# Attention scores issued for two heads at a time in the first stage of a two-layer decoder

## The reference, cut to what matters

```python
def _L0_attn_ref(x, Wq, Wk, Wv, rel_bias_table, ln_gamma, ln_beta):   # H = 16 heads of 8
    q, k, v = (einsum('bsd,ed->bse', x, W) split into heads for W in (Wq, Wk, Wv))
    attn = softmax(einsum('bhqd,bhkd->bhqk', q, k) * d_model ** -0.5)
    attn = attn + rel_bias[None]
    out = einsum('bhqk,bhkd->bhqd', attn, v), heads joined
    return layernorm(out) * ln_gamma + ln_beta
x = x + _L0_attn_ref(_layernorm(x), ...)
```

## Time and profile before

| | us |
|---|---|
| median of three timed runs | 643.53 |
| profiled execution | 639.99 |
| its span, first to last instruction | 638.0 |
| TensorE matmul busy in it | 542.6 (85%) |
| VectorE, ScalarE, GpSimd busy | 421.6, 327.5, 193.3 |

### The profile page before, as it was taken

The page is one execution under the profiler, slowest core; times in us unless marked ns, Lnnn a source line. Parts: engine busy times, 40 slices in busy tenths (PEclk is TensorE's granted clock), DMA queues, the critical chain, the costliest instruction groups (busy, mean ns, idle before and its releaser), DMA issues. The chain is left out here.

```text
span 638.0 us, 12873 instructions
## 1 busy us (share of the span) xinstructions
PE 542.6 (85%) x4890; PEld 334.9 (53%) x4890; DVE 421.6 (66%) x1037; ACT 327.5 (51%) x809; POOL 193.3 (30%) x288
## 2 busy tenths in 40 slices
PE   1777888999999999778896479988997989999995
PEld 1533344344555656455464355665665766655553
DVE  5595674642563554788559865757556567689894
ACT  1424355556577574586642535553664547363440
POOL 3554200312263443332620031001113122335663
PEclk9875799999999999889998789999998999999997
DMA  8600000000030000000166005300000000300301
GB/s 289 258 2 2 2 3 3 1 3 2 1 134 0 2 1 1 2 2 1 43 174 234 1 2 165 103 3 2 4 3 2 3 3 1 134 2 0 133 2 33
DMA packets 25815, 27.92 MB, mean 44 GB/s; under 512 B 18177, under 2 KB 22794, under 8 KB 24858
## 3 DMA queue, kind: packets, MB, share of 16 engines
q1 hardware_dynamic: 25754, 27.10, 12.7%
HBM read 22.14 MB, written 4.75 MB: 42 GB/s over the span
## 5 line engine op out<-in xcount | busy, mean ns | idle before, releaser
L785 POOL TENSOR_TENSOR A_l0x_prob<-A_l0x_prob,A_l0x_inverted_sums 128x256 f32<-128x256 f32 (+1 forms) x32 | 26.2, 840 | 61.7 <-DVE A_l0x_inverted_sums L896 61.7
L785 POOL TENSOR_TENSOR B_l0x_prob<-B_l0x_prob,B_l0x_inverted_sums 128x256 f32<-128x256 f32 (+1 forms) x32 | 27.1, 868 | 46.6 <-DVE B_l0x_inverted_sums L896 46.5
L879 DVE TENSOR_REDUCE A_l0x_nmax<-A_banks 128x2 f32<-128x256 f32 (+1 forms) x32 | 16.3, 551 | 26.9 <-PE A_banks L954 26.9
L2054 PE MATMUL A_banks<-A_moe_xT,w_moe_rows 128*128 128x512 f32 x72 | 34.0, 599 | 0.0
L2054 PE MATMUL B_banks<-B_moe_xT,w_moe_rows 128*128 128x512 f32 x72 | 33.3, 599 | 0.0
L299 DVE TENSOR_REDUCE B_l0a_nmax<-B_banks 128x2 f32<-128x512 f32 x32 | 21.4, 686 | 17.4 <-PE B_banks L226 17.3
L299 DVE TENSOR_REDUCE A_l0a_nmax<-A_banks 128x2 f32<-128x512 f32 x32 | 21.4, 685 | 12.0 <-PE A_banks L226 11.8
L333 ACT ACTIVATE A_l0a_expT<-A_banks 128x512 f32<-128x512 f32 x32 | 18.5, 599 | 21.0 <-PE A_banks L263 21.0
L803 ACT ACTIVATE B_l0x_prob<-B_banks,B_l0x_nmax 128x128 f32<-128x128 f32 x64 | 26.0, 421 | 6.0 <-DVE B_l0x_nmax L879 6.0
L803 ACT ACTIVATE A_l0x_prob<-A_banks,A_l0x_nmax 128x128 f32<-128x128 f32 x64 | 26.0, 427 | 1.2 <-DVE A_l0x_nmax L879 1.2
L820 ACT ACTIVATE B_l0x_probT<-B_banks 128x384 f32<-128x384 f32 x32 | 15.8, 493 | 21.0 <-PE B_banks L966 21.0
(11 more groups left out here) (610 smaller groups left out, 1605.1 us busy)
## 6 DMA issues: line engine op xcount, KB each, us to landing
w_toeplitz_rows<-in_toeplitz_rows SPq DMA_DIRECT2D x1, 3072.0 KB, 15.8
w_moe_rows<-in_moe_rows SPq DMA_DIRECT2D x1, 2304.0 KB, 8.8
w_l1x_rows<-in_l1x_rows SPq DMA_DIRECT2D x1, 2048.0 KB, 8.6
A_l1x_values<-A_l1a_v_tokens SPq DMA_DIRECT2D x4, 512.0 KB, 3.2
A_l1x_v_groups<-A_l1x_values SPq DMA_DIRECT2D x16, 128.0 KB, 3.1
B_l1x_values<-B_l1a_v_tokens SPq DMA_DIRECT2D x4, 512.0 KB, 3.4
B_l1x_v_groups<-B_l1x_values SPq DMA_DIRECT2D x16, 128.0 KB, 3.3
w_l0x_vo_rows<-in_l0x_vo_rows SPq DMA_DIRECT2D x1, 1024.0 KB, 8.9
```

Source lines behind the costliest of these rows:

```text
L785: ins = pool.tensor_tensor(pair, pair, bcast(rz[:, g % 2, i, :], 2, n), ALU.mult)
L879: ins = dve.tensor_reduce(nmax[:, b, i, 2 * c:2 * c + 2], lane.banks[:, 0:2, at:at + n], AX, ALU.max, negate=True)
L2054: pe.matmul(hidden_bank(k)[:, :], w["moe_w3" if which else "moe_w1"][:, ORDER[i], part, :], xT[:], start=True, stop=True).then_inc(s_h.sem, 1)
```

## The change

Two new functions issue two heads at a time, and alternate between them: first half of head h, first half of head h + 1, second half of h, second half of h + 1. The two heads lie in opposite row halves and go to two banks. `tensor_S_pair` is used for the first sequence's scores, `tensor_E_pair` for all shifted scores. Each waits once, for both banks. The second sequence's scores keep `tensor_S`. The number of turns per engine and lane stays; a turn that issued the odd head's matmuls now issues none. The table of turns is another one for every engine.

```diff
+    def tensor_S_pair(self, pe, m):
+        if m:
+            pe.wait_ge(*self.s_mx(m))
+        for c in range(SB):
+            for h in (m, m + 1):
+                ins = pe.matmul(self.score_bank(h)[:, c * S:(c + 1) * S], self.q(0, h, c * P, P), self.k(0, h, 0, S),
+                                start=(c == 0), stop=True, skip_group_check=True)
+                if c == SB - 1:
+                    ins.then_inc(self.s_s.sem, 1)
+
+    def tensor_E_pair(self, pe, u):
+        b, h = divmod(u, H)
+        if h == 0:
+            pe.wait_ge(*self.s_q(16 * self.G * (b + 1)))
+        if u:
+            pe.wait_ge(*self.s_p(u))
+        for c in range(SB):
+            for i in range(2):
+                ins = pe.matmul(self.exp_bank(u + i)[:, c * S:(c + 1) * S], self.k(b, h + i, c * P, P), self.q(b, h + i, 0, S),
+                                start=(c == 0), stop=True, skip_group_check=True)
+                if c == SB - 1:
+                    ins.then_inc(self.s_e.sem, 1)
...
-            a.tensor_S(pe, u)
-            if u % 2:
+            if u % 2 == 0:
+                a.tensor_S_pair(pe, u)
+            else:
                 yield
                 transpose_stack(4 * SB + u // 2)
...
-            if n < U:
-                a.tensor_E(pe, n)
+            if n < U and n % 2 == 0:
+                a.tensor_E_pair(pe, n)
...
     "tensor":
-        "A4 W1 A3 W1 A25 B2 A1 B1 A3 B1 A6 B2 A2 B1 A1 B2 A2 B2 A4 B1 A1 B2 A5 B3 A3 B1 ...
+        "A4 W1 A7 W1 A20 B1 A4 B1 A1 B1 A3 B1 A3 B1 A3 B1 A1 B1 A1 B1 A3 B1 A2 B2 A3 B1 ...
     "vector":
-        "A3 W1 A1 W1 A4 W6 A3 B1 A4 B1 A1 B1 A15 B1 A13 B1 A2 B3 A2 B1 ...
+        "A3 W1 A1 W1 A2 W1 A2 W2 A2 W2 A1 W1 A5 B1 A1 B1 A1 B1 A11 B1 A15 B1 A1 B3 A4 B1 ...
     "gpsimd":
-        "A12 B3 A4 B13 A10 B2 ...
+        "A12 B1 A3 B2 A1 B13 A11 B1 ...
     "sync":
-        "A1 W13 B1 A2 B2 L1 ...
+        "W3 A1 W10 B1 A2 B2 L1 ...
```

More of the change, by code:

```diff
@@ L2358 @@
     "tensor":
[7 rows of a table removed]
-    "vector":
[8 rows of a table removed]
-    "scalar":
[4 rows of a table removed]
[8 rows of a table added]
+    "vector":
[9 rows of a table added]
+    "scalar":
[5 rows of a table added]
     "gpsimd":
-        "A12 B3 A4 B13 A10 B2 A2 B3 A4 B1 A1 B1 A1 B1 A2 B1 A1 B2 A2 B1 A1 B7 A3 B2 A3 B2 A1 B8 A8 B3 A3 B3 A1 B1 A2 B3 A1 B2 A2 B2 A2 B1 A10 B4 A1 B10 A1 B2",
+        "A12 B1 A3 B2 A1 B13 A11 B1 A1 B1 A1 B2 A1 B1 A2 B1 A1 B1 A1 B1 A2 B1 A1 B2 A2 B1 A1 B6 A1 B2 A1 B1 A3 B2 A1 B1 A1 B7 A8 B2 A2 B2 A1 B2 A2 B2 A1 B3 A1 "
+        "B1 A1 B2 A7 B1 A4 B3 A1 B1 A1 B9 A1 B1 A1 B2",
     "sync":
-        "A1 W13 B1 A2 B2 L1 A6 L1 A3 B7 A1 B3 A2 B2 A1 B1",
+        "W3 A1 W10 B1 A2 B2 L1 A6 L1 A3 B5 A1 B5 A2 B2 A1 B1",
 }
```

## The result

| | before | changed |
|---|---|---|
| median of the timed runs, us | 644.13 (643.41 to 645.62, 4 runs) | 619.78 (619.46 to 621.6, 4 runs) |
| profiled execution, its span | 639.99, 638.0 | 619.47, 617.5 |
| TensorE's mean granted clock in it | 0.946 | 0.954 |

The ratio is 0.9625 (95% interval 0.9598 to 0.9652): 24 us faster, where 4 were forecast and 10 were the end of the range. VectorE, ScalarE and GpSimd are as busy as before (424.6, 323.5 and 192.1 us); TensorE is busy 529.0 us for 542.6. For the experiments further down, medians are those of all executions, while ratios compare only executions within 1.5% of the fastest of their kernel, so the two don't divide into each other.

What follows compares the result with a forecast made beforehand. TensorE was taken to bound the kernel from 112 us on. 3.6 - 1.0 - 0.5 + 1.5 = 3.6 us off 643.53 gave 640.0 us; range 638 to 642, 8 in 10 within 634 to 647.

Steps and rivals of the forecast that it cites:

- (c): Every engine's turns re-ordered through the whole program: 1.5 us gained at the start, 0 later than 170 us.
- the rest of the table: Turns later than 170 us: same code, small shifts, sign unknown; 0 us, bounds of 5 us either way.
- if the lead changes after 170 us, the table is the cause: Sign in the changed trace: work from 170 us on should keep the same lead of 3 to 4 us.
- The start: Lane A's opening turns, before its scores: it can begin its scores earlier, 1.5 us gained, upper bound 3.31.
- the cover that I counted on: Lane A's first scores: VectorE must still do sixteen reductions, so 1.5 us was taken, not the upper bound 3.31.
- (a): First-stage scores on TensorE: two heads alternated in a pair share places, 3.6 us gained, bounds 0 and 6.4.
- (b): First-stage scores: a pair waits for both banks; 1.0 us lost at A's reductions (gap 0.47 for 0.24), 0.5 at exponentials.
- The loss of a second bank: Rival, lane A's first scores and its loop from 52 to 110 us: 4.9 us slower, 648.4 us; chance 0.10.
- ScalarE's idle time: Sign before the first stage's exponentials: 21.0 and 14.3 should stay or fall; growth over 5 means lost banks decide.
- Hidden already: Rival, first-stage scores: the chip already overlaps adjoining heads, a gain of 1 meets a loss of 1, 643.5 us; chance 0.14.
- the table gains more: Rival: the start gives 3.3 us, the places after 170 us some 2 more, 636 us; chance 0.20.
- the 3.5 us between the profiled execution and the timed median: Whole run: the timed median 643.53 lies 3.5 us above the profiled 639.99; the same gain was taken from it.

Runs made afterwards that it cites:

- e7: The kernel before, single heads, with the new table of turns only behind lane B's first stage: 629.04 us, ratio 0.9722.
- e3: The changed kernel with the new table only up to the end of lane B's first stage, the old table behind: 634.01 us, ratio 0.9871.
- e5: The changed kernel and its table, but each pair's heads issued one after the other, each waiting for its own bank: 623.63 us, ratio 0.9697.
- e13: The kernel before with new turns up to lane A's first scores and again behind lane B's first stage: 625.26 us, ratio 0.9777.
- e9: The kernel before with new turns only from 170 to 345 us: 644.6 us, ratio 0.9996.
- e10: The kernel before with new turns only from about 440 us to the end: 637.29 us, ratio 0.9985.
- e11: The kernel before with new turns only from 300 to 345 us: 644.99 us, ratio 1.0104.
- e14 to e17: The kernel before, new turns only from 170 to 450, 170 to 400, 330 to 400, 350 to 400 us: ratios 0.994, 0.996, 1.013, 1.004.

## Why the prediction was wrong

The step that failed is (c), the table of turns. "Of the rest of the table, later than 170 us, I cannot tell the sign [...] I take 0, with bounds of one expert step of the tail either way": alone, with the old code, it gave 8.5 us at equal clock and 13.9 in the means (e7), outside that bound. I read "the code there is the same and turns shift mostly by one to five places" as small. Of the 20 us of lead 14 are made behind 170 us; e7 gains 12.2 there by those shifts alone, and e3, with the old turns there, 2.6. The bound came from the tail's idle time, 7.7 us, which I rounded down to 5 and which says nothing of the stages ahead of the tail; the bound to take for a gain was at least the idle time of TensorE in the whole stretch, 438 - 385.8 = 52 us. Even this leaves out a way to gain: of e7's gain only 4.2 us are idle time, and 7.9 are busy time, which shrank with more of the stretch at the higher clock. I had named the sign for it ("if the lead changes after 170 us, the table is the cause"), and so it is.

The start was mis-sized as well: 1.5 for a measured 4.6. I priced L2174 and named the casts, and took half of the one, whose 3.31 us were the clock of that execution (2.00 in others of the same program); the load of x (1.2 measured) got no term of its own, and the cover that I counted on ("VectorE must still do sixteen reductions") only moved earlier with them: they begin at 26.32 instead of 31.96.

Part (a), 3.6 gained, less (b), 1.5 lost: by their signs in the trace right (pairs start together, gap 0.48 for 0.47), in the time 1.0 us with the old table. With the new one, alternation and the common wait give nothing measurable (e5), and pairs and their own turns together 3.0 at most (e13); how these 3.0 divide stays open. Why (a) gave less than 3.6 no run shows; half of its 3.5 us for lane A and for B's first scores was counted although TensorE waits there, and five of the pairs that I priced at 0.32 as standing apart followed directly, 0.20 to 0.24 behind their partners. The loss of a second bank did not decide, and ScalarE's idle time fell in lane B and grew by 1.0 in lane A. "Hidden already" was the best of my rivals for the pairs. The 39 places of 0.12 us that went, 4.7 us, are about the most that (a) could have given. That the rival "the table gains more" had the right sign is no more than that: it priced the later turns at 2.

The Trainium skill's rule that matmuls start strictly in program order ("TensorE: Matmul & The Clock Gate", Part 3, The mechanism) is contradicted by e5 as it was by the earlier trace rows: L262 of two heads starts at 82.98 with L263 of the first standing between them in the program. Its advice to rotate independent groups through banks ("Perfetto Trace Analysis", Optimizing Tensor Performance, Matmuls) shows in the gap, 0.25 us where each bank is waited for by itself and 0.48 where two are waited for together, and not in the time.

Last, the basis. I took the 3.5 us between the profiled execution and the timed median as a constant to carry over. The profiled execution's 640.0 us at a clock of 0.946 lie near the line (639.5), and 643.5 where it has 0.938; so it is most likely the granted clock, which moves single executions by more than my whole forecast.

## What to carry to other kernels

Where engines run two programs by a fixed order, a new order is a change to the whole kernel: what it can gain is to be looked for in the idle time of the fullest engine over everything it covers, and in its clock, not in the size of the shifts. Gains in neighbouring stretches need not add: here the start and the later stages did, and two parts of the later stages did not, since a part of an order can cost time that the whole wins. Ask of a change in two parts which part touches more of the span. And when the clock differs between executions, compare at equal clock before reading differences of 1%, and ask beside it whether the change itself moves the clock.

## What the runs showed of the hardware

The mean granted clock of one kernel lay anywhere from 0.927 to 0.956, and its time with it from 648 to 634 us. Much of this is made in the first 110 us, where TensorE is often idle. In nine profiled executions whose program is the same up to 170 us (before, e7, e9, e10, e11, e14 to e17) the clock between 32 and 110 us was 0.74 to 0.85, and lane B's first stage ended between 169.8 and 176.2 us; in two executions of the changed kernel it was 0.83 and 0.75, and the lead at the end of the stage 6.2 and 2.2 us. The same sixteen matmuls took 3.31 us in one profiled execution and 2.00 in another, starting 0.21 us apart at the lower level and 0.11 at the higher.

An order of instructions moved the clock too: with the new turns, the same work behind the first stage was done with 22 us at the lower level for 35 (e7 and before), and TensorE was busy 7.9 us less in it.

Two matmuls of 64 rows in opposite row halves start within 0.01 us of each other, also when the first head's second matmul stands between them in the program (82.98 in e5, 81.97 before). In the changed kernel the two heads' four matmuls take 0.39 us (75.14), as one head's two did before (118.81).
